# Layer-1 attention: value products of four chunks issued together on the four column quarters of TensorE

## What is computed

```python
q = rmsnorm(x @ wq_a.T, ...) @ wq_b.T            # 32 heads, 64 plain + 64 rotated features
ckv, k_pe = split(x @ wkv_a.T)                   # 32 latent features, 64 rotated ones
kv = rmsnorm(ckv, ...) @ wkv_b.T                 # k_nope and v of every head, from the 32 latents
scores = einsum('bqhd,bkhd->bhqk', q_full, k_full) * softmax_scale
attn = softmax(where(causal, scores, min))
out = einsum('bhqk,bkhd->bqhd', attn, v).reshape(B, S, H * VD)
return out @ wo.T
```

## Time and profile before

| | |
|---|---|
| time, median of 3 runs | 1667.72 us (1666.61 to 1671.19) |
| profiled execution | span 1666.5 us; the page gives no other time of it |
| PE busy over the span | 1518.7 us (91%) |
| DVE, ACT, POOL busy | 744.5 us (45%), 566.5 us (34%), 621.7 us (37%) |
| attention of layer 1 | 219.6 to 941.0 us, PE busy 712.55 of 721.40 us |
| value products L721, in that stretch | 384 records, 187.7 us busy |

### The profile page before, as it was taken

How to read it: one execution, slowest core, us unless ns; L and a number is a source line. 1 busy time by engine, 2 the same in 40 slices (tenths; PEclk the granted TensorE clock), 3 DMA queues, 4 the chain that set the end, 5 groups by cost and what they waited for, 6 DMA issues and landing times. The chain is left out here.

```text
span 1666.5 us, 25847 instructions
## 1 busy us (share of the span) xinstructions
PE 1518.7 (91%) x8210; PEld 1166.9 (70%) x8211; DVE 744.5 (45%) x1723; ACT 566.5 (34%) x1743; POOL 621.7 (37%) x521
## 2 busy tenths in 40 slices
PE   3999699999999999999999776799999999999960
PEld 1566366666667676666676356799999999999950
DVE  5222565555665565555554657422222222222226
ACT  0322254444554444444444334211111111111114
POOL 0000243334433333343433535726175171571125
PEclk9999799999999999999999989899999999999985
DMA  7033200000000000000000467637286283674337
GB/s 260 26 90 100 76 1 14 9 6 13 13 13 13 13 13 13 13 13 13 13 14 7 182 261 259 220 102 250 74 272 223 88 280 104 214 260 139 101 92 254
DMA packets 66558, 171.50 MB, mean 103 GB/s; under 512 B 6000, under 2 KB 14592, under 8 KB 66192
## 3 DMA queue, kind: packets, MB, share of 16 engines
q0 software_dynamic: 25712, 97.94, 17.8%
q1 hardware_dynamic: 35040, 62.39, 11.3%
q10 hardware_dynamic: 5760, 10.57, 1.8%
HBM read 125.27 MB, written 45.61 MB: 103 GB/s over the span
## 5 line engine op out<-in xcount | busy, mean ns | idle before, releaser
L1588 PE MATMUL bank<-expert_weights,rows_t 128*128 x1872 | 358.9, 347 | 10.6 <-DVE rows_t L1514 10.6
L1588 PEld LDWEIGHTS bank<-expert_weights,rows_t 128*128 128x128 f32 x1872 | 340.3, 189 | 14.3 <-issue 11.2
L921 POOL TENSOR_TENSOR room<-room 128x1024 f32<-128x1024 f32 (+1 forms) x128 | 187.6, 1466 | 429.5 <-DVE room L831 429.5
L891 ACT ACTIVATE room<-bank,room 128x256 f32<-128x256 f32 (+1 forms) x512 | 207.8, 421 | 155.3 <-DVE room L816 155.1
L691 PE MATMUL bank<-room 96*128 (+2 forms) x1024 | 232.3, 347 | 0.0
L721 PE MATMUL bank<-probs_t,room 128*32 128x512 f32 x384 | 187.7, 600 | 0.0
L813 DVE TENSOR_REDUCE room<-bank 128x4 f32<-128x1024 f32 (+1 forms) x128 | 122.4, 956 | 143.4 <-PE bank L693 143.1
L1526 DVE TENSOR_TENSOR x_keep<-x_keep,bank 128x400 f32<-128x400 f32 x78 | 44.5, 571 | 303.4 <-ACT x_keep L1465 302.0
L691 PEld LDWEIGHTS bank<-room 96*128 96x128 f32 x1024 | 156.4, 192 | 30.5 <-issue 4.2
L1020 POOL TENSOR_TENSOR expert_weights<-x_keep,expert_weights 128x1600 fp32r<-128x1600 f32 (+2 forms) x49 | 160.2, 3271 | 45.7 <-DMA expert_weights<-w 45.2
L1611 PE MATMUL bank<-expert_weights,act_t 128*128 x702 | 165.6, 389 | 1.0 <-ACT act_t L1470 1.0
(11 more groups left out here) (241 smaller groups left out, 1989.6 us busy)
## 6 DMA issues: line engine op xcount, KB each, us to landing
x_keep<-w POOLq DMA_DIRECT2D x28, 800.0 KB, 4.9
expert_weights<-w POOLq DMA_DIRECT2D x28, 800.0 KB, 6.3
x_keep<-w POOLq DMA_DIRECT2D x14, 768.0 KB, 5.3
expert_weights<-w POOLq DMA_DIRECT2D x14, 768.0 KB, 6.6
rows_by_expert<-room SPq DMA_DIRECT2D x1, 9984.0 KB, 29.9
x_keep<-rows_by_expert SPq DMA_DIRECT2D x39, 256.0 KB, 3.7
results_by_row<-x_keep ACTq DMA_DIRECT2D x39, 256.0 KB, 5.1
room<-wo SPq DMA_DIRECT2D x16, 512.0 KB, 5.3
```

The source lines that it names most:

```text
L891: last = sc.activation(Pr[:, m % 4, hh, 0:w], scores_bank(m)[:, w * hh:w * hh + w], ACT.Exp, bias=nb[:, par, hh:hh + 1], scale=SCALE, accu ...
L921: g.tensor_tensor(pr, pr, rs[:, one[1] % 2].unsqueeze(2).broadcast_to([P, 4, w]), ALU.mult).then_inc(normed, 1)
L1588: last = mm(psum(2 * hf + w)[:, 0:HF], xgT[:, par, of_x, P * k:P * k + P], W[:, ds(off + (of_w * SLOT + (k * 2 + w) * FF + hf * HF), HF)], ...
```

## The change

The value products of four chunks are issued together, in the step that has the last of them as m-3 (m = 6, 10, 14 and 2 of the next sequence). For one key tile the four products go to quarters 0, 1, 2, 3 in turn; for two key tiles this is done for kt = 0 and then for kt = 1, added in the same quarters. The turned probabilities wait for this in a ring of eight slots. In TensorE's step the value products now stand ahead of `turn_p`, since `turn_p` leads to writes into ring slots that they read. `pv_done` counts groups of four. `OT` holds one query tile in place of two.

```diff
             s.OT = sb(scope, "out_latent_parts", [P, 2, 8 * P], F32R)
-            s.PT = sb(scope, "probs_t", [P, 2, 2, 4 * P])
+            s.PT = sb(scope, "probs_t", [P, PT_RING, 4 * P])
...
+    def pt_slot(m, kt):
+        return m % 8 if m < 8 else (m % 4) * 2 + kt
...
-        def values(self, b, m, n):
+        def values(self, b, g, n):
             pe = self.pe
+            last_m = 4 * g + 3
             pe.wait_ge(p_out, n + 1)
-            if kw(m) == SEQ:
-                pe.wait_ge(k1_out, b * 8 + (m - 8) + 1)
-            if m % 4 == 0 and not (isinstance(n, int) and n < 4):
-                pe.wait_ge(o_low, b * 4 + m // 4)
-            if m == 0:
+            if kw(last_m) == SEQ:
+                pe.wait_ge(k1_out, b * 8 + (last_m - 8) + 1)
+            if not (isinstance(n, int) and n < 4):
+                pe.wait_ge(o_low, b * 4 + g)
+            if g == 0:
                 pe.wait_ge(v_staged, b + 1)
-            j = m % 4
-            for kt in range(kw(m) // P):
-                last = nc.tensor.matmul(psum(7)[32 * j:32 * j + 32], cks[:, kt], PT[:, m % 2, kt],
-                                        start=(kt == 0), stop=(kt == kw(m) // P - 1))
+            tiles = kw(last_m) // P
+            for kt in range(tiles):
+                for j in range(4):
+                    last = nc.tensor.matmul(psum(7)[32 * j:32 * j + 32], cks[:, kt], PT[:, pt_slot(4 * g + j, kt)],
+                                            start=(kt == 0), stop=(kt == tiles - 1))
             last.then_inc(pv_done, 1)
...
+        three = behind(3)
+        if three and (live or m < 3) and three[1] % 4 == 3:
+            w.values(three[0], three[1] // 4, n - 3)
         two = behind(2)
         if two and (live or m < 2):
...
             w.turn_p(two[1], n - 2, 0)
-        three = behind(3)
-        if three and (live or m < 3):
-            w.values(three[0], three[1], n - 3)
         if chunk_turned(b, m, live):
             w.turn_q(b, m, n)
...
-                dve.wait_ge(pv_done, b * 16)
+                dve.wait_ge(pv_done, b * 4)
...
-            act.wait_ge(pv_done, n - 2)
+            act.wait_ge(pv_done, three[0] * 4 + three[1] // 4 + 1)
```

More of the change, by code:

```diff
@@ L37 @@
 NBLK = 2 * NB * SEQ // P + E - 1
+PT_RING = 8
 CONSTS = {}
@@ L160, in build @@
             s.qs = sb(scope, "q_latent_parts", [P, 2, 2, P], F32R)
-            s.OT = sb(scope, "out_latent_parts", [P, 2, 2, 8 * P], F32R)
+            s.OT = sb(scope, "out_latent_parts", [P, 2, 8 * P], F32R)
             s.gate = sb(scope, "gate_tiles", [P, 2, D])
-            s.PT = sb(scope, "probs_t", [P, 2, 2, 4 * P])
+            s.PT = sb(scope, "probs_t", [P, PT_RING, 4 * P])
             normalise_latents(s)
@@ L730, in project @@
                 for i in range(8):
-                    last = nc.tensor.matmul(psum(6), OT[:, of_o, qt, P * i:P * i + P], s.Wo[:, of_w, i],
+                    last = nc.tensor.matmul(psum(6), OT[:, of_o, P * i:P * i + P], s.Wo[:, of_w, i],
                                             start=(p == 0 and i == 0), stop=(p == 2 and i == 7))
@@ L834, in dve_step @@
             dve.wait_ge(p_turned, n - 1)
-            v.tensor_copy(PT[:, two[1] % 2, 0], psum(5)).then_inc(p_out, 1)
+            v.tensor_copy(PT[:, pt_slot(two[1], 0)], psum(5)).then_inc(p_out, 1)
         three = behind(3)
@@ L840, in dve_step @@
             half_of = slice(4 * P * (three[1] // 4 % 2), 4 * P * (three[1] // 4 % 2 + 1))
-            v.tensor_tensor(OT[:, LOW, three[1] // 8, half_of], psum(7), OT[:, HIGH, three[1] // 8, half_of],
-                            ALU.subtract).then_inc(o_low, 1)
+            v.tensor_tensor(OT[:, LOW, half_of], psum(7), OT[:, HIGH, half_of], ALU.subtract).then_inc(o_low, 1)
         if tile is not None:
@@ L876, in act_step @@
             act.wait_ge(k1_turned, two[0] * 8 + two[1] - 8 + 1)
-            sc.activation(PT[:, two[1] % 2, 1], psum(4), ACT.Copy).then_inc(k1_out, 1)
+            sc.activation(PT[:, pt_slot(two[1], 1)], psum(4), ACT.Copy).then_inc(k1_out, 1)
         if live:
@@ L897, in act_step @@
         if three and (live or m < 3) and three[1] % 4 == 3:
-            act.wait_ge(pv_done, n - 2)
-            qt, hf = three[1] // 8, three[1] // 4 % 2
-            sc.activation(OT[:, HIGH, qt, 4 * P * hf:4 * P * hf + 4 * P], psum(7), ACT.Copy).then_inc(o_out, 1)
+            act.wait_ge(pv_done, three[0] * 4 + three[1] // 4 + 1)
+            hf = three[1] // 4 % 2
+            sc.activation(OT[:, HIGH, 4 * P * hf:4 * P * hf + 4 * P], psum(7), ACT.Copy).then_inc(o_out, 1)
         if m in (5, 13) and not (first and m == 5) or (not live and m == 3):
```

## The result

The changed kernel takes 1587.9 us (median; 1587.0 to 1588.4) against 1668.5 us for the kernel before in the same measurement: ratio 0.9506, 95% interval 0.9493 to 0.9518, so 80.6 us or 4.9% less. The forecast was 1569, range 1551 to 1610.

What follows compares the result with a forecast made beforehand. PE was taken to bound the attention: 1666.5 us span, less 134.7 (180.5 of value products removed, 45.8 added), plus 20.2 and 16 of lost cover, gives 1568.0; the median lies 1.2 above the span, so 1569, range 1551 to 1610.

Steps and rivals of the forecast that it cites:

- The price of a group: Value products on PE: 16 groups at 1.00 us and 16 at 1.86 us, 45.8 us added.
- B: Rival for the value products: only neighbouring matmuls overlap, groups take 2.27 and 3.99 us; 1618 us, chance 0.03.
- C: Rival for the value products: quarters run one after another, groups take 3.56 and 7.00 us; 1692 us, slower, chance 0.03.
- The cover for bank 4: Before `turn_q`, PE waits for ACT's copy of the kt = 1 probabilities: 56 x 0.36 = 20.2 us.
- The cover for the chain behind the scores: DVE additions in the first query tile now reach PE through POOL's wait: 2.0 us a sequence, 16 us.
- In the second query tile the slack swallows them: Second query tile: 0.32 us of slack before `turn_q` absorbs DVE's additions, so they cost PE nothing.
- The write at m = 2 and the copy at m = 3: DVE's low part of `OT` and latents' copy in the first query tile: together 0.55 us a sequence.
- 0.8 us for steps 7 and 8: Residual and statistics behind the projection at m = 5 delay DVE: about 0.8 us a sequence.
- The step was a good guide: Old trace's one step with `turn_p` but no value product, b = 0, m = 2: 0.33 us lost.
- rival E: PE's granted clock in the attention falls from 1.00 to 0.86: some 1620 us, chance 0.03.
- A: Rival: ACT's copy and the chain hide in full, 1533 us, 1551 with half the stalls; chance below 1551: 0.10.
- D: Rival: each step 0.5 us (first query tile) or 0.3 us (second) longer, 51 us; 1592 to 1625, chance 0.14.

Runs made afterwards that it cites:

- E5: Kernel before with one edit, DVE's reciprocal ahead of the rotation of the queries: ratio 0.9998 to the kernel before.
- E4: Changed kernel with a two-tile group's products issued quarter by quarter, its key tiles one after the other: 1585.9 us, ratio 0.9488.
- E3: Changed kernel with value products in 64 groups of two chunks in place of 32 groups of four: 1609.7 us, ratio 0.9645.
- E2: Changed kernel with the kt = 1 probabilities turned into bank 7, not bank 4, at m = 11, 12, 13, 15, 0, 1: 1575.4 us, ratio 0.9429.
- E6: Changed kernel with the low part of OT written one step later: 1607.0 us on a second, slower chip, ratio 0.9444 to the kernel before there.
- E10: Changed kernel with only the projection moved from bank 6 to bank 7: ratio 0.9455 to the kernel before.
- E1: Changed kernel with DVE's reciprocal of chunk m-1 ahead of the rotation of the queries: 1579.4 us, ratio 0.9463.
- E7: Changed kernel with the edits of E1 and E10 together: ratio 0.9365 to the kernel before.
- E8: Changed kernel with the edits of E1, E10 and E2 together: ratio 0.9291 to the kernel before.
- E9: E8 with the OT write one step later, bank 7 taking the kt = 1 probabilities only at m = 12, 13, 0, 1: ratio 0.9287 to the kernel before.

## Why the prediction was right, and where it was off

**What bounds, and what is removed.** Right. PE set every step before (E5: nothing changes when the chain behind the scores gets shorter), and the value products took 22.5 us of a sequence's 89.93.

**The price of a group.** Right to 0.01 us: 0.99 for four products and 1.85 for eight, taken as 1.00 and 1.86 from L503. The rivals in which quarters do not or only partly overlap (B, C) are refuted by these rows, and E4 refutes the mechanism of B, by which four records of a quarter in a row would have cost most. The Trainium skill's sentence that a weight load passes a running matmul only for another row group ("TensorE: Matmul & The Clock Gate", Part 3) does not describe this case: all quarters share the row groups, and the trace does not agree with it. In the group at 573.38 the eight weight loads start and end within 0.16 us, while its first products, which start at 573.38 and take 0.62 us, are running:

```profile
573.37 0.16 PEld L727 LDWEIGHTS bank<-probs_t,room 128*32 128x32 f32 x8 [0.26 <-issue]
```

What the same part says first, that small products placed on different tiles of the array run concurrently, and that a column tile's output stands in PSUM partitions 32j to 32j + 32, does agree: 0.99 us for four against 0.98 for one, and E3 shows the same for two.

**The cover for bank 4.** Right in place, count and nearly in size. The trace has 56 waits of L683 for L882, and P grew by 0.43 us, as a mean of the eight steps of a sequence, against 0.36 forecast (619.37 to 620.61 and 0.1 make 1.34 and not 1.33, so the rows give 0.38): 3.4 us instead of 2.9. E2 shows that it is the shared bank: where the bank is another, P is back at 0.87 to 0.93.

**The cover for the chain behind the scores.** The step of the sum that was mis-sized. I had 2.0 us a sequence, 16 us in all; the table has 3.6 us, 29 in all. I had also named the wait for the wrong end of the chain. The slack was worked out for `turn_q`, which waits for POOL's L928; but 1.9 of the 3.6 us stand ahead of `turn_p`, which waits for POOL's multiply (14 us on PE in the group rows above). Three terms of it were wrong:

- "In the second query tile the slack swallows them": it does not. For `turn_p` the same rows give 0.23 + 4.44 (618.98 to the end of L921 at 623.42) + 0.05 = 4.72 us against PE's 0.62 + 0.96 + 0.48 + 2.09 + 0.62 = 4.77: hardly any slack where I had 0.32, and 0.4 more only by the wait for bank 4. At the seam the scores are 0.84 us shorter, which turns this into 0.4 us of wait, and the `OT` write at m = 14 makes the maximum of step 15 late by another 0.5. I had 0.15 us for this seam; it was 0.9 (C and S at m = 0). E6, without that write, leaves 0.35.
- The write at m = 2 and the copy at m = 3 were put at 0.55 us. Ahead of and behind `turn_p` of m = 4 PE lost 0.75.
- The projection waits for DVE's rotation to leave bank 6. It was on no list of mine, and costs 0.55 us at m = 4 and 0.15 at m = 12. E10 shows it. In E1 it grew and hid much of that edit's gain.

What I put at 0.8 us for steps 7 and 8 was 0.8 (C and P at m = 7 and 8). The step was a good guide: 0.77 and 0.69 us there, 0.77 and 0.69 at m = 7. That is luck in part: in the earlier trace rows DVE's scaling took 0.47 us in place of 0.17 (last section), besides the 0.2 us that I named.

**What was not in the sum.** The 0.09 us for entering the quarters, 12 times less a sequence: 9 us of gain that hid part of the error. In the rows it was there to be read, as P0.53 beside Q0.48, but I had the whole 0.12 us inside the value product's 0.98.

**The rest.** 8 x (7.0 - 1.1) = 47 us of the 50.4 lost in the attention (134.7 - 84.3). The other 3 are in the last sequence, to the next stage's first product: 103.9 us before and 95.8 after, 8.1 less where the others are 10.9 less. Its second query tile has no next queries and from m = 9 on no `turn_q`, and behind the last scores PE waits for POOL and then works at less clock:

```profile
838.78 1.16 PE L709 MATMUL bank<-ident_sb,room 128*128 128x128 f32 x8 [3.75 <-POOL room L926]
...
843.60 3.31 PE L727 MATMUL bank<-probs_t,room 128*32 128x512 f32 x16 [0.78 <-DVE probs_t L841]
```

```profile
840.00:850.00 10.00, 6.80 (x31) 3.47 (x32) 2.06 (x3) 1.24 (x3) 0.73 (x1) 0.68 0.00 0
```

The same wait was 0.96 us in the kernel before, and the granted clock was 1.00 there from 920 to 930 us. The group of 16 records has a duration of 3.31 us in this place and of 1.92 elsewhere. So what rival E feared did happen here, over some ten microseconds and behind a wait longer than the 1.5 us that I foresaw; from 220 to 820 us the granted clock stayed at 1.00. A (no cover needed) did not happen. Nor did D (the chain as the bound of every step): in steps 2, 3, 5, 6 and 9 PE waits for nothing, in 1, 10, 11, 13 and 14 for ACT's copy alone, and the chain costs time in 0, 4, 7, 8, 12 and 15. With the 3.8 us of later start, the profiled execution makes 1666.5 - 84.3 + 3.8 - 0.7 = 1585.3.

## What to carry to other kernels

Small products into the four quarters of a bank (here 32 by 512 columns, float32) are worth grouping: four take the time of one, two also, and the order among them hardly matters. But before long instructions are taken out of a saturated engine, list every wait of the instructions that follow them and work out each from start to start, shared banks too; here 56 of 135 us came back as such waits (8 x 7.0). Work it out for every instruction that waits, not only for the last one in the chain. And an edit that removes a wait must be read step by step: it may only reach the next one, as E1 did, and three such edits together gave 4.9 us a sequence where the largest alone gave 1.5.

## What the runs showed of the hardware that I had not expected

A short DVE instruction on SBUF operands, the scaling of the maximum, takes longer when POOL is in an operation: mean 173 ns before, 226 ns in the changed kernel, up to 634 ns. Group of the changed kernel and timeline of one case:

```profile
L822 DVE TENSOR_SCALAR room<-room 128x4 f32<-128x4 f32 x128 | 28.9, 226 | 4.4
```

```profile
387.60 0.72 POOL L933 TENSOR_TENSOR room<-room 128x256 f32<-128x256 f32 x1
...
387.73 0.62 DVE L822 TENSOR_SCALAR room<-room 128x4 f32<-128x4 f32 x1
388.26 0.55 DVE L870 TENSOR_TENSOR room<-bank,consts_sb 128x384 f32<-128x384 f32 x1
```

It starts at 387.73 and ends at 388.35, just after POOL's operation (388.32). All 23 that took over 0.2 us start within an operation of POOL and end 0.03 us behind it. With shorter steps this meets more often: 6.8 us more on DVE in all (28.9 against 22.1). DVE's split of queries at m = 9 shows the same in E1, E5, E7, E8 and E9: 1.25 us in place of 0.28, beside POOL's multiply. The long scalings stand at m = 0, 4 and 10; that at m = 4 (0.62 us) comes right before the rotation for which PE then waits ahead of the projection. Its share in PE's waits was not tried by itself.
